# Delta-rule attention block, projections: the short filter on ACT and DVE, one square for a unit, and the last silu behind the next unit's first evictions

## The reference, cut to what matters

```python
q = silu(_causal_dwconv(x @ Wq, conv_q))      # 4 taps, a channel at a time
k = silu(_causal_dwconv(x @ Wk, conv_k))
v = silu(_causal_dwconv(x @ Wv, conv_v))
fs = _fir(vh, fir_short)                      # 3 taps, a channel at a time, causal
_l2norm(x) = x * rsqrt(sum(x * x, -1, keepdims=True) + 1e-6)    # q and k, over the 64 channels of a head
```

## Time and profile before

| | us |
|---|---|
| median of 3 runs | 2887.21 |
| lowest and highest | 2874.64 and 2901.07 |
| profiled execution | 2885.66 |
| its span in the trace | 2883.4 |
| the projections in it | 134.6 to 460.0 |
| PE, DVE, ACT, POOL busy over the span | 2573.3, 1657.3, 1117.0, 607.6 |

### The profile page before, as it was taken

How to read it: one execution, slowest core, us unless ns; L and a number is a source line. 1 busy time by engine, 2 the same in 40 slices (tenths; PEclk the granted TensorE clock), 3 DMA queues, 4 the chain that set the end, 5 groups by cost and what they waited for, 6 DMA issues and landing times.

```text
span 2883.4 us, 40407 instructions
## 1 busy us (share of the span) xinstructions
PE 2573.3 (89%) x13824; PEld 1813.5 (63%) x13824; DVE 1657.3 (57%) x4330; ACT 1117.0 (39%) x2286; POOL 607.6 (21%) x420
## 2 busy tenths in 40 slices
PE   4899993338898899967999999999999999999998
PEld 3456663336787788844666665666666666666665
DVE  4488783216940455525655755675566657665764
ACT  1478874328655222212333333323333333333321
POOL 1145552012100111012111212220221122122210
PEclk8999997765859999977999999999999999999999
DMA  4544557768846778521011101110110111011000
GB/s 117 180 135 157 168 167 199 185 146 202 202 116 171 218 221 249 151 74 44 8 45 52 52 1 52 52 37 16 52 53 6 46 52 52 1 51 51 8 1 15
DMA packets 349601, 274.03 MB, mean 95 GB/s; under 512 B 166412, under 2 KB 306124, under 8 KB 347876
## 3 DMA queue, kind: packets, MB, share of 16 engines
q1 hardware_dynamic: 337680, 256.90, 30.8%
q0 software_dynamic: 3456, 12.58, 1.7%
q10 hardware_dynamic: 8276, 2.10, 0.4%
HBM read 170.65 MB, written 100.89 MB: 94 GB/s over the span
## 4 chain that ended last, share of the span: by engine, by line
PE 38%; DVE 8%; POOL 8%; issue 3%; DMA 0%; POOLq 0%; ACT 0%; DVEq 0%; SPq 0%; ACTq 0%
PE mx_dn L1828 13%; PE mx_up L1814 11%; POOL mx_st L1714 4%; PE mx_m L1767 4%; DVE mx_acc L2119 3%; PE mx_m L1768 2%; PE mx_m L1776 2%; PE mx_m L1791 2%; POOL mx_rms L1725 2%; DVE mx_t L1981 1%; PE mx_m L1805 1%; POOL mx_acc L1732 1%; PE mx_m L1777 1%; POOL mx_acc L1735 1%; DVE mx_t L1983 1%
## 5 line engine op out<-in xcount | busy, mean ns | idle before, releaser
L2119 DVE SCALAR_TENSOR_TENSOR mx_acc<-mx_dn,mx_comb,mx_acc 128x256 f32<-128x256 f32 x1024 | 424.4, 477 | 478.6 <-PE mx_dn L1828 476.5
L1828 PE MATMUL mx_dn<-mx_edn,mx_hs 128*128 128x256 f32 x2048 | 512.7, 395 | 3.3 <-ACT mx_hs L1897 3.3
L1828 PEld LDWEIGHTS mx_dn<-mx_edn,mx_hs 128*128 128x128 f32 x2048 | 397.5, 197 | 168.3 <-issue 95.2
L1814 PE MATMUL mx_up<-mx_h2T,mx_eup 128*128 128x512 f32 x1024 | 497.9, 609 | 0.0
L1897 ACT ACTIVATE mx_hs<-mx_up 128x512 f32<-128x512 f32 x320 | 189.9, 596 | 793.4 <-PE mx_up L1814 793.0
L1814 PEld LDWEIGHTS mx_up<-mx_h2T,mx_eup 128*128 128x128 f32 x1024 | 189.8, 192 | 156.9 <-issue 147.7
L669 DVE SCALAR_TENSOR_TENSOR cv_acc<-cv_pre,conv_w,cv_acc 128x512 f32<-128x512 f32 x288 | 215.6, 750 | 78.0 <-ACT cv_acc L591 71.2
L533 PE MATMUL cv_pj<-cv_hT,wqkv 128*128 128x512 f32 x384 | 181.2, 602 | 13.0 <-ACT cv_acc L591 8.0
L1719 POOL TENSOR_TENSOR mx_t<-mx_vf,mx_ids 128x1024 f32<-128x1024 f32 x16 | 31.5, 1966 | 650.1 <-DVE mx_pr L1976 650.1
L1108 PE MATMUL ci_gps<-ci_kT 64*128 64x128 f32 x768 | 101.1, 426 | 48.9 <-DMA ci_kT<-kqT_d 42.0
L823 PE MATMUL fl_ps<-fl_toep,fl_vc 128*84 128x98 f32 x512 | 56.7, 280 | 92.8 <-DMA fl_toep<-taps_d 46.9
(11 more groups left out here) (232 smaller groups left out, 4296.9 us busy)
## 6 DMA issues: line engine op xcount, KB each, us to landing
kqT_d<-cv_kqc SPq DMA_DIRECT2D x16, 1024.0 KB, 8.1
vf_d<-cv_vf SPq DMA_DIRECT2D x16, 1024.0 KB, 5.3
ds_kqT<-kqT_d SPq DMA_DIRECT2D x16, 1024.0 KB, 5.8
mx_vf<-vf_d SPq DMA_DIRECT2D x16, 1024.0 KB, 6.2
fl_toep<-taps_d SPq DMA_DIRECT2D x32, 392.0 KB, 5.4
ci_kT<-kqT_d POOLq DMA_DIRECT2D x24, 512.0 KB, 5.6
fl_pool<-vf_d SPq DMA_DIRECT2D x8, 1216.0 KB
xin<-_attn_hidden_states_dram SPq DMA_DIRECT2D x16, 512.0 KB, 4.2
```

Of the source, the lines that this page charges most:

```text
L1814: ins = pe.matmul(up_ps[x % 2][:], lhs, h2T[i][:, k, :], start=(k == 0), stop=(k == KD - 1))
L1828: ins = pe.matmul(dn_ps[(i + n) % 2][:, j, :], hs[x % 4][:, j * P:(j + 1) * P], rhs, start=(x == 0 and j % 2 == 0) or x >= NS, stop=(x >= ...
L2119: ins = dve.scalar_tensor_tensor(out=acc[i][:, j, :], in0=dn_ps[(i + n) % 2][:, j, :], scalar=comb[i][:, j, e:e + 1], in1=acc[i][:, j, :], ...
```

## The change

The short filter is no longer made on PE. ACT makes its last tap from `vT` into a new buffer `ff` (`last_tap`), DVE adds the two others (`fir`), between the conv taps of slots 1 and 2, and PE only transposes the result. Only k is turned by token, in two halves of two tiles (`turn_k`), and ACT copies 512 columns at a time. ACT squares k and q of a unit in one operation by channel (`square`), PE sums over the channels of a head with matmuls against a matrix `pick` of two columns (`sum_sq`), DVE adds epsilon from PSUM (`add_eps`), POOL takes one power of 32 columns. On ACT the silu of block 5, the square, `vhalo` and the two last taps are taken out of the unit's last slot and stand as `rest` behind slot 0 of the next unit; `turn_v` moves to slots 3 to 5. `diag_fs` and its six products are gone; the semaphores of `norm_inputs` are cleared along with those of `setup`.

```diff
             def turn_v(u, g, j):
                 i = g % 2
                 if j == 0:
-                    pe.wait_ge(silu_done, u * NBLK + (NBLK + 3))
-                    pe.wait_ge(vhalo_done, u + 1)
+                    pe.wait_ge(fir_done, u * KD + KD)
                 pe.wait_ge(vfe_done, u * J + (j + 1))
...
                 for k in range(KD):
-                    for t in range(FIRS):
-                        ins = pe.matmul(vf_ps[j % 2][:, D + k * P:D + (k + 1) * P], vT[i][:, k, c0 + t:c0 + t + P],
-                                        m.diag_fs[:, k, t, :], start=(t == 0), stop=(t == FIRS - 1))
+                    ins = pe.transpose(vf_ps[j % 2][:, D + k * P:D + (k + 1) * P], ff[i][:, k, c0:c0 + P], m.ident[:])
                 ins.then_inc(vf_done, 1)

-            def turn_kq(u, g, j):
...
+            def turn_k(u, g, y):
+                if y == 0:
+                    pe.wait_ge(silu_done, u * NBLK + (NKQ + 3))
+
+                pe.wait_ge(k_done, u * 2 + (y + 1))
+                for j in two:
+                    c0 = (2 * y + j) * P
+                    for k in range(KD):
+                        ins = pe.transpose(k_ps[y][:, j * D + k * P:j * D + (k + 1) * P],
+                                           kqc[g % 2][:, k, c0:c0 + P], m.ident[:])
+                ins.then_inc(kt_done, 1)
+
+            def sum_sq(u, g, j):
+                i = g % 2
                 if j == 0:
+                    pe.wait_ge(sq_done, u + 1)
+                    pe.wait_ge(eps_done, u + 1)
+                for a in range(NKQ):
+                    ins = pe.matmul(ss_ps[i][:, j * 2 * H + a * 2:j * 2 * H + a * 2 + 2], sq[i][:, a, j * P:(j + 1) * P],
+                                    pick[:], start=True, stop=True)
+                if j == J - 1:
+                    ins.then_inc(ss_done, 1)
...
                 for s in range(NBLK):
                     if nxt is not None:
                         project(nxt, g + 1, s)
-                    if s < J:
-                        turn_kq(u, g, s)
-                    if 1 <= s < J + 1:
-                        turn_v(u, g, s - 1)
+                    if s < 2:
+                        turn_k(u, g, s)
+                    if 1 < s < 4:
+                        sum_sq(u, g, 2 * s - 4)
+                        sum_sq(u, g, 2 * s - 3)
+                    if s >= 3:
+                        turn_v(u, g, s - 3)
+                    if s == NBLK - 1:
+                        turn_v(u, g, J - 1)
...
+            def square(u, g):
+                i = g % 2
+                act.wait_ge(silu_done, u * NBLK + (NKQ + 3))
+                act.activation(sq[i][:], kqc[i][:], ACT.Square).then_inc(sq_done, 1)
+
+            def last_tap(u, g, k):
+                i = g % 2
+                act.wait_ge(silu_done, u * NBLK + (NKQ + k + 4))
+                act.activation(ff[i][:, k, :], vT[i][:, k, FIRS - 1:], ACT.Copy, scale=m.fs_w[:, k, FIRS - 1:FIRS])\
+                    .then_inc(tap_done, 1)

             def front_slot(u, g, s):
                 evacuate(u, g, s)
                 if s >= 1:
                     silu(u, g, s - 1)
                 if s == NBLK - 1:
-                    silu(u, g, s)
                     halo(u, g)
-                    vhalo(u, g)
+
+            def rest(u, g):
+                silu(u, g, NBLK - 1)
+                square(u, g)
+                vhalo(u, g)
+                for k in range(KD):
+                    last_tap(u, g, k)
...
                 for s in range(NBLK):
-                    if s < J:
-                        act.wait_ge(kq_done, u * J + (s + 1))
-                        act.wait_ge(red_done, u * J + (s + 1))
-                        act.activation(k[i][:, s, :], kq_ps[s % 2][:, 0:D], ACT.Copy).then_inc(k_done, 1)
-                        act.activation(sq[s % 2][:], kq_ps[s % 2][:], ACT.Square).then_inc(sq_done, 1)
+                    if s < 2:
+                        act.wait_ge(kt_done, u * 2 + (s + 1))
+                        act.activation(k[i][:, 2 * s:2 * s + 2, :].rearrange("p j c -> p (j c)"), k_ps[s][:], ACT.Copy)\
+                            .then_inc(k_done, 1)
                     if nxt is not None:
                         front_slot(nxt, g + 1, s)
-                    if 1 <= s < J + 1:
-                        act.wait_ge(vf_done, u * J + s)
-                        act.activation(vf[i][:, s - 1, :], vf_ps[(s - 1) % 2][:], ACT.Copy).then_inc(vfe_done, 1)
+                    if s == 0:
+                        rest(u, g)
+                    if s >= 3:
+                        put_vf(u, i, s - 3)
+                    if s == NBLK - 1:
+                        put_vf(u, i, J - 1)
...
                     ins.then_inc(conv_done if t == CONV - 2 else conv_step, 1)
-
-            def reduce_sq(u, j):
...
+                    if between is not None and t < CONV - 2:
+                        between(t)
+
+            def fir(u, g, k, t):
+                i = g % 2
+                if t == 0:
+                    dve.wait_ge(tap_done, u * KD + (k + 1))
+                    dve.wait_ge(vhalo_done, u + 1)
+                else:
+                    dve.wait_ge(fir_step, u * KD + (k + 1))
+                dve.scalar_tensor_tensor(out=ff[i][:, k, :], in0=vT[i][:, k, t:t + UT], scalar=m.fs_w[:, k, t:t + 1],
+                                         in1=ff[i][:, k, :], op0=ALU.mult, op1=ALU.add)\
+                    .then_inc(fir_done if t == FIRS - 2 else fir_step, 1)
+
+            def add_eps(u, g):
+                i = g % 2
+                dve.wait_ge(ss_done, u + 3)
+                dve.wait_ge(rn_done, u + 1)
+                dve.tensor_scalar(ss[i][:], ss_ps[i][:, 0:J * 2 * H], L2_EPS, None, ALU.add).then_inc(eps_done, 1)
...
                 for s in range(NBLK):
-                    if 1 <= s < J + 1:
-                        reduce_sq(u, s - 1)
+                    taps = None
+                    if 1 <= s < 1 + FIRS - 1:
+                        taps = lambda t: fir(u, g, t, s - 1)
                     if nxt is not None:
-                        conv(nxt, g + 1, s)
+                        conv(nxt, g + 1, s, taps)
+                    elif taps is not None:
+                        for k in range(KD):
+                            taps(k)
+                    if s == NBLK - 2:
+                        add_eps(u, g)
...
-            for s in m.setup_sems:
+            for s in m.early_sems:
                 pool.sem_clear(s)
```

More of the change, by code:

```diff
@@ L225, in _ @@
             n = 8 + B * KD
-            for k in range(KD):
-                for t in range(FIRS):
-                    dve.tensor_scalar(m.diag_fs[:, k, t, :], m.ident[:], fs_w[:, k, t:t + 1], None, ALU.mult)\
-                        .then_inc(vec_step, 1)
-            n += KD * FIRS
             dve.wait_ge(act_step, 4)
@@ L261, in sem @@
         def sem(name):
-            return ctx.enter_context(nc.semaphore(name))
+            m.early_sems.append(ctx.enter_context(nc.semaphore(name)))
+            return m.early_sems[-1]
         xin = [sb(f"xin{i}", [P, J, D]) for i in range(UB)]
@@ L633, in front, with put_vf @@
                     front_slot(u, g, s)
+            def put_vf(u, i, j):
+                act.wait_ge(vf_done, u * J + (j + 1))
+                act.activation(vf[i][:, j, :], vf_ps[j % 2][:], ACT.Copy).then_inc(vfe_done, 1)
             def body(u, g, nxt):
@@ L658, in _, with conv @@
             dve.sem_inc(k_done, 2)
-            dve.sem_inc(sq_done, 2)
-            def conv(u, g, o):
+            dve.sem_inc(ss_done, 2)
+            def conv(u, g, o, between=None):
                 i = g % 2
@@ L695, in _, with body @@
         def _(pool):
-            def body(u):
-                for j in range(J):
-                    pool.wait_ge(red_done, u * J + (j + 3))
-                    pool.tensor_tensor(ss[j % 2][:], ss[j % 2][:], m.l2_eps[:, 0:2 * H], ALU.add)\
-                        .then_inc(eps_done, 1)
-                    pool.wait_ge(eps_done, u * J + (j + 3))
-                    pool.tensor_tensor(m.rn[:, bass.ds(u * (J * 2 * H) + j * 2 * H, 2 * H)], ss[j % 2][:],
-                                       m.half_pow[:, 0:2 * H], ALU.pow).then_inc(rn_done, 1)
-            with pool.Fori(0, NU) as u:
-                body(u)
+            pool.memset(pick[:], 0.0).then_inc(pick_done, 1)
+            pool.wait_ge(pick_done, 1)
+            for hh in two:
+                pool.memset(pick[hh * DK:(hh + 1) * DK, hh:hh + 1], 1.0).then_inc(pick_done, 1)
+            def body(u, i):
+                pool.wait_ge(eps_done, u + 3)
+                pool.tensor_tensor(m.rn[:, bass.ds(u * (J * 2 * H), J * 2 * H)], ss[i][:], m.half_pow[:, 0:J * 2 * H],
+                                   ALU.pow).then_inc(rn_done, 1)
+            with pool.Fori(0, NU // 2) as t:
+                for i in two:
+                    body(t * 2 + i, i)
 def long_filter(nc, m, w):
```

46 lines of the change are left out of this document (21 added, 25 removed).

## The result

| | before | after |
|---|---|---|
| median (lowest to highest), 12 runs each | 2888.19 (2852.41 to 2915.97) | 2934.45 (2907.82 to 2942.97) |
| profiled execution, span | 2885.66, 2883.4 | 2938.97, 2937.0 |
| projections begin | 134.6 | 135.5 |
| last silu of unit 0 and of unit 15 | 157.59, 445.06 | 158.79, 500.26 |
| one unit, mean of 15 | 19.16 | 22.77 |

The change makes the kernel 1.8% slower: the ratio is 1.0176, 95% interval 1.0141 to 1.0211 (the ratios of this document leave disturbed executions out, so they can differ slightly from the quotient of the medians). All of it is in the projections, 325.4 us before and 383.7 after, 58.3 more. The stages behind give back 5.6, nearly all in the experts' stage, which is the same code.

A forecast was written before the change was run, and what follows sets the result against it. Before, DVE's hole and PE's nearly full time set the unit; after, a closed loop of waits among ACT, DVE and PE. Loop +30.3, tail -0.9, setup -1.2 on 2885.66 made 2914; falling clock +14 made 2928 us, range 2899 to 2954.

The forecast's parts named there:

- The moved hole: DVE's idle 2.97 us ahead of a unit's block 0 moves behind block 0 and stays about as long.
- The loop through the turn: Projections: ACT, DVE and PE wait in a circle, block 4's projection behind v's turn; period 21.23 us, +30.3 in all.
- 5 x 0.748: DVE's time for block 1 or 2 with two short-filter taps between its filter operations: 3.74 us.
- A: Start on ACT of a unit's last silu, which can't be before DVE is done with the last block.
- The second hole: DVE idle ahead of block 4, waiting for the projection that stands behind v's turn on PE: 0.76 us.
- The clock: TensorE falls to half speed around block 4's turn and projection: 1.2 us in 12 of 15 units, +14 us.
- Rival (a): Projections: the loop of waits with TensorE's clock kept up, total 2914 us; chance 0.22.
- Small matmuls: PE's 32 recorded sums of squares of 2 columns per unit take 0.106 us each, 3.4 us.
- The tail: From the last unit's last silu to the vf store's issue, 10.07 us before: change of -0.9 us.
- Setup and clears: Dropping six diagonal products on DVE shortens the setup by 1.2 us; 19 more semaphore clears on POOL cost nothing.
- Rival (d): Projections: DVE's hole is really closed, a unit takes 17.1 us, total 2853 us; chance 0.08.
- Rival (b): The loop, half speed lasting into block 5 and the next unit's projections: 15 x 3.1 us, total 2960; chance 0.12.

The follow-up runs named there:

- Experiment 3: The changed kernel with the square over 8 of the 512 tokens of each block, so norms are not computed: median 2904.24 us, ratio to before 1.0116, unit 20.58.
- experiment 2: The changed kernel with filler matmuls of 256 columns on PE, two behind the first sums and five behind the last: median 2920.11 us, ratio to before 1.0112, unit 20.76.
- 7: The changed kernel with v turned in pairs in slots 4 and 5, block 4's projection ahead of the turns: median 2907.55 us, ratio to before 1.0071, unit 21.04.
- experiment 1: The changed kernel with five filler matmuls of 256 columns on PE behind each unit's sums of squares: median 2946.99 us, ratio to before 1.0218, unit 21.45.
- Experiment 9: The kernel of experiment 8 with the last unit reordered, square ahead of the last silu, all sums ahead of v's turns: median 2869.63 us, ratio to before 0.9975.
- experiment 8: The changed kernel with ACT's block spread over several slots, square in halves, v turned in pairs: median 2868.89 us, ratio to before 0.9963, unit 18.16.
- 10: The kernel of Experiment 9 plus one filler matmul of 256 columns ahead of each unit's first 16 sums: median 2864.05 us, ratio to before 0.9969, unit 17.80.

## Why the prediction was right, point by point

**The moved hole: right.** ACT's block from the last silu to DVE's block 1 was predicted at 5.34 and is 278.09 - 272.75 = 5.34. The hole is 2.85 against 2.97 before. Experiment 3 shows it is on the path. The square's 1.92 (mean 1.916), worked out from a wider row and a rate, was exact; the power was put at 5.6 and is 5.57, hidden as said.

**The loop through the turn: right, a little long.** Experiments 2 and 7 show it with the clock up: 20.66 a unit, and 1.0 less with the projection out of the turn's way. I had 21.23. The step that was off is "5 x 0.748": conv and taps alternate between two independent chains and follow each other by 0.665 (278.09, 278.75). The 0.748 is the mean of the three steps of a block, of which two wait for the one before. The last tap was done 11.4 behind A in place of 12.10, and block 4 began 9.80 behind block 1 in place of 10.48. The second hole is 0.85 with the clock up (experiment 2), where I had 0.76; in the changed kernel the slow projection makes it 3.01. Over 15 units the loop came to 7.9 us less than I had.

**The clock: right in kind, too small.** I had 1.2 us in 12 units; it is 2.1 on average in all 15, 31.6 in place of 14. Two things were off. In the unit shown the projection of block 4 ran wholly at half speed, 3.62 against 1.88, and 0.4 of block 5 besides (2.31). And no unit was spared. PE was idle for only 2.50 us ahead of the turn, where I had 3.4, and where the shortest idle time of the earlier trace rows with slow matmuls behind it is 3.42; but ahead of it stood two batches of 16 matmuls of 2 columns with 0.19 and 0.92 of idle time and one projection. So it was in nine of the 15 units. In the six others the clock fell one step earlier, which I had nowhere: block 3's projection, behind the first batch and the 0.92, ran slow already, and the wait ahead of the turn was 0.9 us or less (PE, after):

```profile
252.90 1.95 PE L570 MATMUL cv_ssps<-cv_pick,cv_sq 128*128 128x2 f32 x16 [0.19 <-ACT cv_sq L643]
255.77 3.43 PE L535 MATMUL cv_pj<-cv_hT,wqkv 128*128 128x512 f32 x4 [0.92 <-ACT cv_acc L608]
...
261.93 0.43 PE L546 MATMUL cv_vfps<-ident,cv_vT 128*128 128x128 f32 x2 [0.82 <-DVE cv_ff L722]
```

In five units of experiment 1 it fell at the same place. So the long wait at the turn, on which I rested the fall, is not needed for it. Rival (a), which let the 2-column matmuls hold the clock, was wrong, as the 4-column row of the setup had suggested. How much of the fall is due to these matmuls and how much to the short idle times beside them, no run separates. Over the stage the clock was 0.86, so 0.28 of 22.77, 6.4 us a unit, went by at half speed. The Trainium skill, TensorE: Matmul & The Clock Gate, section "Terms", calls the lower state half-rate, by which 3.2 us of a unit would be lost, by estimate; the measured 2.1 is less, and part of the half-speed time does lie where PE was waiting anyway (281.70 to 284.30: clock 0.84, PE busy for 0.10 of 2.60).

**Small matmuls: right.** 32 records at 0.106 (1.84 for 16 less the drain), not the 62 ns that the Trainium skill, same page, section "Wait — 56ns, not 53.3ns?", gives as the sequencer's time where matmuls are not decoded in hardware. At half speed they take 0.218 (6.99 for 32), as the setup's did.

**The tail: wrong, +4.0 in place of -0.9.** I took the turn of 0.43 to follow the last tap at once. All 32 sums stand ahead of it on PE's queue, and behind 4.34 us of idle time they ran at half speed: 6.99 in place of 3.4. The turn came at 509.59, while the taps were done at 506.2. Experiment 9 mended this by order alone: the tail is 13.8, against 18.9 here and 20.2 in experiment 8, while the last period is 1.9 longer than in 8.

**Setup and clears.** The six products are gone, but DVE had reached them 1.0 later, so that its end moved by 0.17 and not by 1.2; the projections begin 0.9 later. The 19 semaphore clears cost nothing: that stage lasts 299.8 before and 299.6 after.

**The later stages: -5.6**, from the experts' stage (1526.6 and 1520.2 us with the same code and a clock of 0.97 in both). I know no cause beyond the spread between executions. With it the profiled execution of 2938.97 lies 11 above the forecast, and the median 6.5 above; the shorter loop and the faster later stages took back 13.5 of the 24.9 by which start, clock and tail were dearer. That the total came out so near was in part luck; the forecast's total was better than its terms.

**Rivals.** Rival (d), DVE running through, was 5.7 us a unit away (17.1 against 22.77), but experiments 8 and 10 show that the same work reaches 17.8: it failed for their order, not for their work. Rival (b) priced the clock at 3.1 a unit, my forecast at 1.2 in 12 of 15; the measured 2.1 lies between them.

## What to carry to other kernels

Moving an engine's work behind the next unit's first evictions helps only up to the next bound (the silu alone took DVE's hole from 2.97 to 0.79, but the unit only 0.28 down, to PE's work); put five operations there as one block and the hole is only moved. Follow the whole loop, ACT to DVE to PE and back, and break long blocks up between the evictions of several slots; then look for what stands behind each wait on each queue, in the last unit too. And if matmuls of a few columns replace wide ones, look at the granted clock: here it cost 31.6 us against the loop's 22.4, and in the spread version one filler of 256 columns, placed where PE had waited, kept it up.

## What the runs showed that I had not expected

Two independent chains of the same DVE operation, alternating, follow each other by 0.665 us. A step that reads the result of the one before starts about 0.785 behind it: in the kernel before, the block that begins at 275.67 goes on at 276.45 and 277.24, and the reduction, which does not read it, starts at 277.91 (DVE, before):

```profile
276.45 0.75 DVE L669 SCALAR_TENSOR_TENSOR cv_acc<-cv_pre,conv_w,cv_acc 128x512 f32<-128x512 f32 x1
277.24 0.75 DVE L669 SCALAR_TENSOR_TENSOR cv_acc<-cv_pre,conv_w,cv_acc 128x512 f32<-128x512 f32 x1
```

A dependent step thus costs 0.12 more, by estimate 1.4 us over the 12 of them among the 18 filter steps of a unit, though no run here tried to interleave two blocks.

A clock that falls in every third unit, regularly (19.11, 17.80, 17.79, 18.97, 17.80, 17.79, ... in experiment 8), with units whose rows are the same up to the fall: the only idle time that PE's rows show there is 0.45 us ahead of 16 matmuls of 2 columns, and one matmul of 256 columns in its place ended the falls. Why it was every third unit stays open.
